# Moving the first norm of six of eight batches from the prologue into the attention of an adaLN block with a mixture of experts

## The reference, cut to what matters

```python
mod = (silu(c) @ wmod).reshape(8, 6, 1, -1)          # c 8x128, wmod 128x768
sa, ca, ga, sb, cb, gb = (mod[:, k] for k in range(6))   # ga, gb then kept at least 0.25 from zero
h = layernorm(x) * (1 + ca) + sa                     # x: 8 batches x 512 tokens x 128, float32
x = x + ga * attention(h, W_qkv, W_out)              # 16 heads of 64, rotary embedding, causal
h = layernorm(x) * (1 + cb) + sb
x = x + gb * experts(h, gate_w, expert_bias, w_up, w_down)  # 8 experts of 512, top 2; then layernorm + h
```

## Time and profile before

| | us |
|---|---|
| median of 3 runs | 1091.71 (1090.06 to 1092.69) |
| the profiled execution, its own time | 1092.55 |
| its span, first to last instruction | 1090.7 |
| PE busy | 930.5 (85%) |
| DVE busy | 862.0 (79%) |
| ACT busy | 717.5 (66%) |
| POOL busy | 570.1 (52%) |

### The profile page before, as it was taken

The page is one execution under the profiler, slowest core; times in us unless marked ns, Lnnn a source line. Parts: engine busy times, 40 slices in busy tenths (PEclk is TensorE's granted clock), DMA queues, the critical chain, the costliest instruction groups (busy, mean ns, idle before and its releaser), DMA issues. The chain is left out here.

```text
span 1090.7 us, 20160 instructions
## 1 busy us (share of the span) xinstructions
PE 930.5 (85%) x6154; PEld 666.0 (61%) x6154; DVE 862.0 (79%) x1759; ACT 717.5 (66%) x1897; POOL 570.1 (52%) x635
## 2 busy tenths in 40 slices
PE   2369999999999999999999999999996179999800
PEld 1246766676666667666666666666664168887600
DVE  6638888888888888898898788889876469978617
ACT  2237777777777777777777777777774256666504
POOL 2333543643656366555636655563673606767710
PEclk9969999999999999999999999999998579999955
DMA  6022223223222322222232222223122657666334
GB/s 218 20 54 69 55 50 72 50 49 78 55 55 67 82 50 63 76 64 55 65 80 53 63 75 66 55 66 83 45 57 98 242 197 245 237 226 232 125 100 132
DMA packets 67226, 104.26 MB, mean 96 GB/s; under 512 B 11115, under 2 KB 49912, under 8 KB 63536
## 3 DMA queue, kind: packets, MB, share of 16 engines
q1 hardware_dynamic: 59056, 90.53, 28.8%
q0 software_dynamic: 4992, 8.94, 2.5%
q10 hardware_dynamic: 3072, 3.51, 0.9%
HBM read 21.09 MB, written 15.50 MB: 34 GB/s over the span
## 5 line engine op out<-in xcount | busy, mean ns | idle before, releaser
L1093 POOL TENSOR_TENSOR four<-four 128x512 f32<-128x512 f32 x128 | 161.0, 1279 | 329.4 <-DVE ot L1039 201.9
L916 ACT ACTIVATE prob<-ps,nmax 128x512 f32<-128x512 f32 (+3 forms) x512 | 263.9, 529 | 76.3 <-DVE nmax L1016 71.1
L1016 DVE TENSOR_REDUCE nmax<-ps 128x2 f32<-128x1024 f32 (+3 forms) x256 | 211.0, 824 | 8.8
L835 PE MATMUL ps<-ident,prob 128*128 128x128 f32 x1280 | 191.5, 279 | 9.4 <-ACT probt L937 4.2
L835 PEld LDWEIGHTS ps<-ident,prob 128*128 128x128 f32 x1280 | 142.8, 141 | 58.9 <-ACT prob L916 35.3
L1097 POOL TENSOR_TENSOR qk_lo<-four,qk_hi 128x512 fp32r<-128x512 f32 x128 | 162.0, 1287 | 0.0
L857 PE MATMUL ps<-probt,val 128*64 128x512 f32 (+3 forms) x1024 | 153.6, 442 | 0.2 <-ACT probt L937 0.2
L1009 DVE TENSOR_TENSOR ps<-ps,tri 128x256 f32<-128x256 f32 x256 | 109.3, 427 | 49.7 <-PE ps L814 49.1
L944 ACT CAST qk_hi<-four 128x512 fp32r<-128x512 f32 x128 | 79.4, 621 | 99.0 <-POOL four L1093 98.7
L1503 POOL DMA_INDIRECT results<-y,to_i x92 | 103.0, 1119 | 69.2 <-DVE y L1347 44.1
L937 ACT COPY probt<-ps 128x512 f32<-128x512 f32 (+2 forms) x256 | 124.7, 521 | 19.9 <-PE ps L835 17.8
(11 more groups left out here) (215 smaller groups left out, 2176.2 us busy)
## 6 DMA issues: line engine op xcount, KB each, us to landing
four<-four SPq DMA_DIRECT2D x256, 128.0 KB
wt<-wall SPq DMA_DIRECT2D x23, 1024.0 KB
xg<-slots SPq DMA_DIRECT2D x23, 288.0 KB
hb<-h_hi SPq DMA_DIRECT2D x64, 64.0 KB, 2.1
hb<-h_lo SPq DMA_DIRECT2D x64, 64.0 KB, 2.0
y<-results SPq DMA_DIRECT2D x8, 512.0 KB, 7.4
x_all<-in_x SPq DMA_DIRECT2D x4, 512.0 KB, 9.8
h_hi<-rows SPq DMA_DIRECT2D x8, 256.0 KB
```

Source lines behind the costliest of these rows:

```text
L835: mm = e.transpose(ps[:, PT + at % 2, at_block * P:(at_block + 1) * P], prob[:, unit, kk * P:(kk + 1) * P], ident[:])
L916: e.activation(prob[:, unit, 0:w], ps[:, bank_s(idx) + j, 0:w], ACT.Exp, bias=nmax[:, q.par, idx, j:j + 1], accum_out=den[:, q.par, 2 * i ...
L1016: e.tensor_reduce(nmax[:, q.par, idx, :], ps[:, bank:bank + 2, 0:w], AX.X, ALU.max, negate=True).then_inc(v_max, 1)
L1093: e.tensor_tensor(qk[:, cols], tt[:, cols], ur[:, cols], op=ALU.add).then_inc(g_qk, 1)
```

## The change: what it does

The prologue now takes the statistics of tiles 0 to 7 only, and features, h_hi and h_lo of batches 0 and 1 (`FIRST = 2`). DVE, instead of POOL, subtracts `wq_lo`, after normalising batch 1. SP loads the first two `hb` tiles still inside the prologue, after the first h_lo. ACT's copy of `ga` moves behind its two shifts.

At the head of the attention's block DVE takes the statistics of the other 24 tiles and their factors (`n_factors`), and ACT the square root of group 1, before their first slots. For i = 0 to 5 the first norm of batch i + 2 then runs in slots (i, 3) to (i, 5): ACT normalises four tiles into `rows` at (i, 3); at (i, 4) PE transposes them and ACT applies scale and shift into `ht2` and copies the rounded h_hi; POOL subtracts h_lo at the head of (i, 5).

```diff
-RING = 4
+RING = 2
+FIRST = 2
-            for b in range(B):                    # low_parts
+            for b in range(FIRST):
-        SPARE = (0, 2, 6, 7)
+        SPARE = (0, 2, 4, 6, 7)
             # r_norm
+            e.wait_ge(n_tr, min(b + 2, B - FIRST))
             # r_shift
+            e.wait_ge(n_lo, min(b + 2, B - FIRST))
             # spare_read
+            if c == 4 and coming(i) is not None:
+                e.wait_ge(n_ht, i + 1)
             # route_pe
+            if c == 4 and coming(i) is not None:
+                n_turn(e, i)
             # route_act
+            if c == 3 and coming(i) is not None:
+                n_rows(e, i, coming(i))
+            if c == 4 and coming(i) is not None:
+                n_features(e, i, coming(i))
+        minus1 = tmp[:, 3, :]
+        def coming(i):
+            b = i + FIRST
+            return b if i >= 0 and b < B else None
+        def n_factors(e):
+            done, tick = s_dve, first_tick
+            tile_stats(e, NQ, NT)
+            group_begin(e, done, tick, 1, s_st, s_var)
+            group_end(e, done, tick, 1, s_root)
+            n = slice(NQ, NT)
+            e.scalar_tensor_tensor(out=minus1[:, n], in0=mean[:, n], scalar=-1.0, in1=rstd[:, n],
+                                   op0=ALU.mult, op1=ALU.mult).then_inc(n_fac, 1)
+        def n_rows(e, i, b):
+            e.wait_ge(n_fac, 1)
+            if due(i - 2):
+                e.wait_ge(d_xs, 16 * 2 * TB * (i - 2))
+                e.wait_ge(d_h2, 16 * (i - 2))
+            for t in range(TB):
+                m = b * TB + t
+                ins = e.activation(rows[(i + 1) % 2][:, t, 0:E], x_all[:, m, :], ACT.Identity,
+                                   bias=minus1[:, m:m + 1], scale=rstd[:, m:m + 1])
+            ins.then_inc(n_xh, 1)
+        def n_turn(e, i):
+            e.wait_ge(n_xh, i + 1)
+            for t in range(TB):
+                mm = e.transpose(ps[:, BANK_R, t * P:(t + 1) * P], rows[(i + 1) % 2][:, t, 0:E], ident[:])
+            mm.then_inc(n_tr, 1)
+        def n_features(e, i, b):
+            e.wait_ge(n_tr, i + 1)
+            if due(i - 1):
+                e.wait_ge(p_x2, i - 1)
+            e.activation(ht2[:], ps[:, BANK_R, :], ACT.Identity, bias=mod1[:, 0, b:b + 1],
+                         scale=mod1[:, 1, b:b + 1]).then_inc(n_ht, 1)
+            e.wait_ge(n_ht, i + 1)
+            e.copy(h_hi[:, b * S:(b + 1) * S], ht2[:]).then_inc(n_hi, 1)
+        def n_rest(e, i, b):
+            e.wait_ge(n_hi, i + 1)
+            cols = slice(b * S, (b + 1) * S)
+            e.tensor_tensor(h_lo[:, cols], ht2[:], h_hi[:, cols], op=ALU.subtract).then_inc(n_lo, 1)
             # prologue, SP, after its loads
+                    e.wait_ge(s_lo, 1)
+                    load_h(e, 0)
+                    load_h(e, 1)
             # prologue, ACT: group_root(e, 1, ...) gone, ga after the shifts of range(FIRST)
             # prologue, PE: transposes for b in range(FIRST)
             # prologue, DVE
-                    tile_stats(0, NT // 2)
+                    tile_stats(e, 0, NQ)
-                    tile_stats(NT // 2, NT)
-                    group_begin(e, done, tick, 1, s_st, s_var)
-                    for b in range(B + 2):
...
+                    features(0)
+                    features(1)
+                    e.wait_ge(s_whi, 1)
+                    e.tensor_tensor(wq_lo[:], wq_f[:], wq_hi[:], op=ALU.subtract).then_inc(s_wlo, 1)
+                    rounded(0)
+                    rounded(1)
             # prologue, POOL
-                    e.wait_ge(s_whi, 1)
-                    e.tensor_tensor(wq_lo[:], wq_f[:], wq_hi[:], op=ALU.subtract).then_inc(s_wlo, 1)
             # pe_qk
+                if due(q.b - FIRST + 1):
+                    e.wait_ge(n_lo, q.b - FIRST + 1)
             # pool_slot, first thing: n_rest at c == 5
+                route_rest(e, i, c)
             # sp_h: tiles 0 and 1 are not loaded again
+                if x >= 2:
+                    e.wait_ge(p_v, x - 1)
+                    load_h(e, x)
             # attention, ACT, before its first slot
+                    group_root(e, 1, s_var, s_root)
             # attention, DVE, before its first slot
+                    n_factors(e)
```

More of the change, by code:

```diff
@@ L197, in adaln_kernel @@
         modt = sb(rt, "modt", [P, 2, B])
+        mod1 = sb(rt, "mod1", [P, 2, B])
         st4 = sb(rt, "st4", [P, TB, 6])
@@ L224, in adaln_kernel @@
         (d_k, r_ones, r_rs, r_base, r_st, r_f, r_fac, r_xh, p_x1, r_ht, p_x2, r_row, p_lg, r_first, r_expo, r_a, r_hot, r_sum, r_tail,
-         p_pos, r_d, r_slot, d_h2) = (
+         p_pos, r_d, r_slot, d_h2, n_fac, n_xh, n_tr, n_ht, n_hi, n_lo) = (
             sem("r_" + n) for n in (
                 "dk", "one", "rs", "base", "st", "f", "fac", "xh", "x1", "ht", "x2", "row", "lg", "first", "expo", "a", "hot", "sum",
-                "tail", "pos", "d", "slot", "dh2"))
+                "tail", "pos", "d", "slot", "dh2", "nfac", "nxh", "ntr", "nht", "nhi", "nlo"))
         BANK_R = 6
-        SPARE = (0, 2, 6, 7)
+        SPARE = (0, 2, 4, 6, 7)
         def batch(i, back):
@@ L521, in route_dve_last, with route_rest @@
                 r_at(e, b)
+        minus1 = tmp[:, 3, :]
[37 more added lines that the diff above has]
+            e.tensor_tensor(h_lo[:, cols], ht2[:], h_hi[:, cols], op=ALU.subtract).then_inc(n_lo, 1)
+        def route_rest(e, i, c):
+            if c == 5 and coming(i) is not None:
+                n_rest(e, i, coming(i))
         def route_cum(e, i, c):
@@ L557, in adaln_kernel, with load_h, tile_stats @@
         tri = sb(att, "tri", [P, P])
+        hb = [sb(att, f"hb{p}", [P, 2, P], F32R) for p in range(2)]
+        d_hb = (sem("b_dhb0"), sem("b_dhb1"))
+        def load_h(e, x):
+            if due(x // 8 - FIRST + 1):
+                e.wait_ge(n_lo, x // 8 - FIRST + 1)
+            for k, src in enumerate((h_hi, h_lo)):
+                e.dma_start(hb[x % 2][:, k, :].bitcast(F32), src[:, x // 8 * S + x % TB * P:x // 8 * S + x % TB * P + P]
+                            .bitcast(F32)).then_inc(d_hb[x % 2], 16)
+        s_st, s_dve, s_var, s_root, s_mod = (sem("a_" + n) for n in ("st", "dve", "var", "root", "mod"))
+        first_tick = Count()
+        def tile_stats(e, first, last):
+            for n in range(first, last):
+                if n % NQ == 0:
+                    e.wait_ge(d_x[n // NQ], 16)
+                e.bn_stats(stats[:, n, :], x_all[:, n, :]).then_inc(s_st, 1)
         with ExitStack() as ph:
@@ L562, in adaln_kernel @@
             wm = sb(ph, "wm", [P, 6 * E])
-            mod1 = sb(ph, "mod1", [P, 2, B])
             gt = sb(ph, "gt", [B, 2, E])
@@ L566, in adaln_kernel @@
             ht = sb(ph, "ht1", [P, RING, S])
-            (d_c, d_m, d_w, d_i, s_exp, s_silu, s_mm, s_mod, s_rows, s_ga, s_st, s_dve, s_var, s_root, s_xh,
+            (d_c, d_m, d_w, d_i, s_exp, s_silu, s_mm, s_rows, s_ga, s_xh,
              s_tr, s_hi, s_ht, s_lo, s_whi, s_wlo, s_gb, s_num) = (
                 sem("a_" + n) for n in (
-                    "dc", "dm", "dw", "di", "exp", "silu", "mm", "mod", "rows", "ga", "st", "dve", "var", "root",
+                    "dc", "dm", "dw", "di", "exp", "silu", "mm", "rows", "ga",
                     "xh", "tr", "hi", "ht", "lo", "whi", "wlo", "gb",
@@ L601, in _ @@
                     e.copy(wq_hi[:], wq_f[:]).then_inc(s_whi, 1)
[L602 to L605, removed]
                     e.wait_ge(s_mod, 4)
-                    for b in range(B):
+                    for b in range(FIRST):
                         if due(b + 1):
@@ L613, in _ @@
                                      scale=mod1[:, 1, b:b + 1]).then_inc(s_ht, 1)
+                    e.wait_ge(s_gb, 1)
+                    e.copy(ga[:].rearrange("p b f -> p (b f)"),
+                           ps[:, 4:6, :].rearrange("p b f -> p (b f)")).then_inc(s_ga, 1)
                 @block.tensor
@@ L641, in _ @@
                 def _(e):
-                    done, tick = s_dve, Count()
+                    done, tick = s_dve, first_tick
                     e.wait_ge(s_exp, 1)
@@ L683, in _, with features, rounded @@
                     group_end(e, done, tick, 0, s_root)
-                    tile_stats(NT // 2, NT)
-                    group_begin(e, done, tick, 1, s_st, s_var)
-                    for b in range(B + 2):
[L688 to L697, removed]
+                    def features(b):
+                        if due(b - 1):
+                            e.wait_ge(s_tr, b - 1)
+                        normalise(e, b, xh[:, b % 2]).then_inc(s_xh, 1)
+                    def rounded(b):
+                        e.wait_ge(s_ht, b + 1)
+                        e.tensor_copy(h_hi[:, b * S:(b + 1) * S], ht[:, b % RING, :]).then_inc(s_hi, 1)
+                    features(0)
[4 more added lines that the diff above has]
+                    rounded(1)
                 @block.gpsimd
@@ L718, in adaln_kernel @@
```

(12 more changed lines are left out.)

## The result

| | before | after |
|---|---|---|
| median, us | 1090.88 (4 runs, 1089.86 to 1092.69) | 1080.67 (4 runs, 1080.28 to 1082.42) |
| ratio | | 0.9904, 95% interval 0.9884 to 0.9925 |
| the profiled execution | 1092.55 | 1080.80 |
| its span | 1090.7 | 1078.9 |

The change makes the kernel 10.2 us faster by the medians and 11.75 by the profiled pair. Forecast were a gain of 4.7 and a range from 1081.0 to 1091.8; the measured 1080.67 lies just outside it. The sign was right and the size was off by more than a factor of two.

A forecast was written before the change was run, and what follows sets the result against it. Taken as bounds: a chain of batches waiting on each other in the prologue, PE in the attention. 20.0 us gained at the front and 15.3 paid in the attention give -4.7: median 1087.0, range 1081.0 to 1091.8.

The forecast's parts named there:

- Eight fewer start everything behind them 1.69 earlier.: Prologue: eight fewer statistics on DVE at 0.211 us each bring ACT's first root to 15.70 us.
- The rest of the front: Prologue behind the first root: the chain to ACT's first value copy, 15.70 to 33.5 us, with `wq_lo` 3.43 on DVE.
- the gate: Attention's head: ACT's first value copy must wait for group 1's square root, which takes back 4.2 us.
- The price in the attention: Attention: normalising rows costs 1.40 us, transposes, shift and rounding 1.15; 2.55 a batch, times 6, 15.3 paid.
- the first batch: Attention's start: the first moved batch meets a just-filled pipeline and was given the full price of 2.55 us.
- The stages behind the attention: After the attention: only moved in time, with no gain or cost.
- rival 1: Attention: PE's queue swallows ACT's added work, so only 9.7 us are paid; total 1081.4; chance 14%.
- Rival 2: Attention, slot 5: POOL's subtraction holds DVE out, 1.26 us a batch, 7.6 in all; total 1094.6; chance 8%.
- Rival 3: Attention's start: PE's full clock comes later after idling at the head, costing 4 us; total 1091.0; chance 10%.
- upper end: Front: the gain if the statistics run a little denser, 21 us against the 20.0 forecast.

The follow-up runs named there:

- after_again: The changed kernel, unchanged, timed again beside the kernel before: 1086.01 us, ratio 0.986.
- gap_early: The changed kernel with the first norm's ACT normalising and rounding moved into ACT's waits, and 18 head statistics moved to the prologue's end: 1076.32 us, ratio 0.9779.
- after_third: The changed kernel, unchanged, timed once more in the third group beside the kernel before: 1083.91 us, ratio 0.9908.
- before_again: The kernel before, unchanged, timed again beside the kernel before: 1101.56 us, ratio 0.9999.
- first_eight: The kernel before with only 8 tiles of statistics instead of 16 ahead of the factors: 1097.26 us, ratio 0.9973.

## Why the prediction was wrong

- **The step that failed: "Eight fewer start everything behind them 1.69 earlier."** I counted the eight instructions and not what they waited for. In the one trace of before, the first piece of x was late (10.04), and the sixteen statistics ran without a gap behind it; the second piece's wait was hidden behind the first's. What the step takes away is the need for the second piece, which lands at about 12. The root moved by 5.0, not 1.69: 3.3 us, the largest part of the miss (in the profiled pair 11.8 instead of 4.7: 3.45 at the front, 0.9 in the attention, 2.7 behind it). With a late first piece, as in after_again, 2.2 to 2.5 of the 5.0 are left, and there the step as written holds: 5.66 from the first statistics to the root were forecast (10.04 to 15.70), 5.62 measured (9.57 to 15.19). But only 2 of 13 traces have a late first piece; in the others it is the second piece that the kernel before waits for. A row with `x16` under one wait does not show that two transfers were waited for; the code did (`d_x[n // NQ]`).
- **The rest of the front** was right: 17.70 from root to copy, forecast 17.8, and the gate that takes back about 4 was there, as gap_early shows.
- **The price in the attention**: forecast 2.55 a batch by its neighbours, measured 2.7 in the two slots. The sum was forecast at 15.3; the pair of profiles pays 14.4, the means over all traces with and without the additions about 12.5 (0.65 before pair 0's end, 11.8 behind it). The term is 1 to 3 too high: the first batch, given the full price, costs about 1.0, and the slots (i,6) give 1.6 back.
- **The stages behind the attention**, held at zero, gave 2.7 in the profiled pair. They take between 252 and 260 us over all traces, without regard to the change. That is not a step of the change, but it belonged into the width of the range.
- **The rivals.** The time of rival 1 (1081.4) came nearly true by luck, for a reason that is not its own: ACT's work was not swallowed, PE stood 1.21 and 0.44 for it. Rival 2 did not occur: DVE's reciprocal, the small SBUF instruction closest to `n_rest`, took 0.19 to 0.21 us in all 64 pairs, the routing's products kept their length (`share` 347 ns in the mean, 345 before), and the subtraction ran where POOL waited. Rival 3 did not either, and its price was wrong. In both traces of before the clock granted to PE stands at half (1.2 GHz) from about 62 to 79 us. In the trace of after it never leaves the full 2.4 GHz there. This is the stretch that answers to 68 to 84 of the earlier trace rows; the clock is the third figure from the end:
```profile
45.60:61.60 16.00, 12.57 (x65) 8.89 (x64) 10.86 (x18) 9.53 (x28) 5.39 (x5) 1.00 0.24 57
```
In after_third, the same program, it is at half from about 38 to 46 us and again from 52 to 54. From the first value copy to the end of pair 0 that trace took 36.2 us, the two at full clock 37.1 and 37.0, before 36.0: a half clock in this stretch cost nothing that can be read, where the prediction gave it 4.
- **The range** began at the rival's 1081.0 and left nothing below for the front, whose upper end I had set at 21; with the wait for the second piece counted it would have been about 24.

## What to carry to other kernels

Before pricing work that leaves a chain, list the transfers it waits for, not only its instructions: one trace shows only the wait that happened to end last, and moving the work can remove a dependency that never showed. The end of an in-order engine's program for a slot is not free room, even when the engine is only 75% busy: what counts is which instruction is queued behind and who waits for it. The same four instructions cost 1.5 us before exponential 5 and, two and two, about 0.1 before exponential 0. Where a neighbour in the same loop already does such work, its price per pair is a better estimate than any sum of durations, and it points to a second gain: the neighbour can move as well.

## What the runs showed of the hardware that was not expected

- The landing of the first 512 KB transfer of a program varies between two levels in executions of the same kernel, while ACT's 1.5 MB load of weights runs beside it: DVE could start on it at 5.9 to 6.4 us in eleven traces and at 9.6 and 10.0 in two.
- Eight single-input `TENSOR_SCALAR` instructions on DVE took 8.63 us instead of 2.14 while POOL subtracted two SBUF tensors, because one of them took 6.84; eighteen statistics instructions beside POOL's subtraction of h took 3.57, no longer each than with POOL quiet (24 in 4.74).
- The stages behind the attention, which no kernel here changed, took 252 to 260 us, and the level goes with the group of runs, each on another chip: 252.3 to 252.4 in one, 257.5 to 258.2 in another. No run isolates the cause.
- At the start of the attention the granted clock of PE stands at half for about 17 us in all three traces of kernels with the long prologue (before, before_again, first_eight). Of the ten with the short one, six keep the full clock there and four do not; after is one of the six and after_third, the same program, one of the four.
